# Attention and expert kernel: ScalarE presets the score banks with minus the row maxima

## Chip, cores and metric

One core of one Trainium2 chip. The time is device microseconds (us) of one execution of the whole program. Runs of the kernel before: 915.74, 917.42 and 919.55 us, median 917.42.

## What is computed

One transformer block in fp32, on x of 2 batches x 1024 tokens x 128 features: a modulated layer norm, attention with 16 heads of 64 (queries and keys over 64 latents, rotated by position), gates, a second layer norm, and an expert layer (8 experts, each token by one of its two best). The change lies in the attention alone:

```python
h = _layernorm(x, axis=-1) * (1 + ca) + sa
q = _apply_rope_subspace((c_q @ w_up_q.T) ..., DR)
k = _apply_rope_subspace((c_kv @ w_up_k.T) ..., DR)
scores = jnp.einsum('bhqd,bhkd->bhqk', q, k) * scale
attn = jax.nn.softmax(scores, axis=-1)
out = jnp.einsum('bhqk,bhkd->bhqd', attn, v)
out = out @ w_out.T + residual
```

## The kernel before

**Pairs, halves, steps.** The attention works through 16 pairs of heads (8 for each batch). A pair has 16 steps: two halves of 512 queries, and in each half eight tiles of 128 keys. Two steps are a group, so that a pair has eight groups, 0 to 7. Nothing schedules the work: each engine has its own queue, written out by hand in nested loops over p (pair) and g (group), and the queues meet through named semaphores.

**One group on TensorE.** `maxima(p + 1, 2g)` multiplies 128 queries of the next pair with 512 keys for both heads, into the two banks of `ps_m` (L411), for VectorE to reduce. `score(p, 2g)` and `score(p, 2g + 1)` each fill two banks of `ps_s`, scores transposed, keys on partitions: for both heads k_hi by q_hi (L429), k_lo by q_hi (L431), k_hi by q_lo (L433), and a row product (L435), ones by the row `neg_row`, that subtracts from each query its maximum. The first head lies on partitions 0 to 63 and the second on 64 to 127, so that the products come in twos. Then `maxima(p + 1, 2g + 1)`, `up(p + 2, g)` (L399, a quarter of a later pair's q or k), and `pv` for the two steps before (L445, probabilities by latent values, into `ps_o`). Steps of even number use banks 0 and 1 of `ps_s`, the odd ones banks 2 and 3.

In groups 3 and 7 there follow `denominators` (L453, ones by the sums of probabilities, into bank 2 of `ps_s`) and `outputs` (L462, of the pair before, into bank 3), which wait until `expo` has read the step's scores. So step 1 or 9 behind them waits until ScalarE has read the denominators and VectorE has added the outputs to `x_sb`.

**The other engines.** VectorE, in a group: `reduce_max` (L1082) of the first maxima, `lower` (L1075, the lower bits of the q or k quarter of the group before, which frees its banks for `up`), `reduce_max` of the second maxima, `turn` (L1064 to L1069, rotation). In groups 0 and 4 it begins with `out_add` (L1135) and ends with `recip` (L1121); in groups 3 and 7 it has `neg_max` (L1087, minus the maximum of a half's queries, in `nm`); in groups 2 and 6 `divide` (L1126). `maxima` waits until the reduction before has emptied `ps_m`; `up` waits for `lower`. ScalarE: `upper` (L676, a cast), `expo` twice (L684, the exponential of two banks, 128x1024), `den_out` (L696) at the start of groups 0 and 4, `o_out` (L691) at their end. GpSimd adds each step's probabilities (L930).

**SyncE's queue.** For each half, `max_rows` (L1377) sends the eight columns of `nm`, 128 numbers each, to `neg_row` by eight DMAs. `den_cols` (L1385), `inv_rows` (L1390) and `inv_spread` (L1395) take the denominators of a half to columns for `recip`, and the inverses over HBM to all partitions for `divide`. The queue is in order: `max_rows(p, 1)`, `den_cols(p - 1, 0)` and what follows it, `max_rows(p + 1, 0)`, `den_cols(p - 1, 1)` and what follows.

In pair 14 nothing is left for `up`, and in pair 15 nothing for `maxima`; there VectorE also has the second layer norm and the choice of experts for batch 0. The expert layer comes last.

Of the kernel before, what the change touches and what calls it, by code (L numbers as in the profile page):

```python
# [46 lines left out]
def build(nc, t, out):  # L47
    ctx = ExitStack()
    with ctx:
# [6 lines left out]
        def sem(name):  # L56
# [35 lines left out]
        one_row = sb("one_row", [P, P], F32R)  # L92
        neg_row = sb("neg_row", [P, 2, S], F32R)
# [3 lines left out]
        nm = sb("nm", [P, 2, 2, 4], F32R)  # L97
# [10 lines left out]

        rd_dram = nc.dram_tensor("rd_dram", [2, 2, HALF], F32, kind="Internal").ap()
# [97 lines left out]
            "scores": "both heads' scores of a step, less the maximum (tensor)",  # L207
# [38 lines left out]
        row_placed = [sem(f"row_placed{n}") for n in range(2)]  # L246
# [94 lines left out]
        def _(pe):  # L341
# [73 lines left out]
            def score(p, st):  # L415
# [4 lines left out]
                ge(pe, s["probs"], n_step(p, st) - 2)  # L420
                if kt == 0:
                    pe.wait_ge(row_placed[half], 128 * (p + 1))
                if kt == 1:
                    ge(pe, s["den_read"], n_part(p, half) - 2)
                    ge(pe, s["out_added"], n_part(p, half) - 3)
                kc, qc = slice(kt * P, (kt + 1) * P), slice(half * HALF, (half + 1) * HALF)
                bank = [ps_s[:, 2 * (st % 2) + h, :] for h in range(2)]
                for h in range(2):
                    nc.tensor.matmul(bank[h], k_hi[rows(h), p % 3, kc], q_hi[rows(h), p % 3, qc], start=True, stop=False)  # L429
                for h in range(2):  # L430
                    nc.tensor.matmul(bank[h], k_lo[rows(h), p % 3, kc], q_hi[rows(h), p % 3, qc], start=False, stop=False)  # L431
                for h in range(2):
                    nc.tensor.matmul(bank[h], k_hi[rows(h), p % 3, kc], q_lo[rows(h), p % 3, qc], start=False, stop=False)  # L433
                for h in range(2):
                    ins = nc.tensor.matmul(bank[h], one_row[rows(h), :], neg_row[rows(h), p % 2, qc], start=False, stop=True)  # L435
# [20 lines left out]
            def outputs(p, half, bank):  # L456
# [67 lines left out]
            for p in range(NPAIR):  # L524
                for g in range(NGRP):
# [95 lines left out]
        def _(act):  # L621
# [64 lines left out]

            def o_out(p, half):
# [60 lines left out]

            for p in range(NPAIR):
# [786 lines left out]
```

## Time and profile before

| | |
|---|---|
| median of three runs | 917.42 us |
| the profiled execution's own time | 909.34 us |
| its span, first to last instruction | 907.6 us |
| TensorE matmul busy | 818.4 us (90%), 5118 instructions |
| VectorE busy | 641.9 us (71%) |
| ScalarE busy | 394.1 us (43%) |
| GpSimd busy | 663.3 us (73%) |
| mean granted TensorE clock | 0.946 of full |
| chain that ended last: TensorE's part | 78% |

The span is what lies between the first and the last instruction of the profiled execution; that execution took 909.34 us, 1.7 us more than its span, and 8.1 us less than the median of the three runs without a profile. Busy time on TensorE is the union of its matmuls' times, whose ends are modelled. The attention lies between about 78 and 792 us; the expert layer follows.

### The profile page before, as it was taken

The page shows a single profiled execution, that of the slowest core. Times are in us where ns is not written, and L with a number is a line of the kernel's source. Part 1 is how long each engine was busy: PE and PEld are TensorE (multiplying, and loading weights), DVE is VectorE, ACT ScalarE, POOL GpSimd, SP SyncE. Part 2 cuts the span into 40 slices and gives each one's busy share as a digit, 9 for nine tenths or more (in the row PEclk, how much of TensorE's full clock was granted, in tenths as well). Part 3 has the DMA queues.
Part 4 walks back from the last instruction along what each step waited for, and adds up shares of the span by engine and source line. Part 5 has one row for each costly group of instructions (what it writes and reads, how often), then busy time and mean ns, then how long its engine had stood idle before and what let it go on. Part 6 is the DMA issues. An engine that isn't in the chain of part 4 may idle for free.

```text
span 907.6 us, 14678 instructions
## 1 busy us (share of the span) xinstructions
PE 818.4 (90%) x5118; PEld 489.8 (54%) x5118; DVE 641.9 (71%) x1156; ACT 394.1 (43%) x644; POOL 663.3 (73%) x350
## 2 busy tenths in 40 slices
PE   3678999999999999999999999999999977959591
PEld 1435555555555555555555555555555434448581
DVE  7877777777777777777777777777777767536023
ACT  2443444444444444444444444444444324326351
POOL 3684988888878787878788787878778866532433
PEclk8776999999999999999999999999999989869796
DMA  7200001010101010101011111010010100068693
GB/s 194 79 1 13 13 13 25 13 25 14 24 14 25 14 25 13 24 14 24 14 24 14 25 13 25 13 26 14 13 13 13 24 13 1 13 211 273 212 328 88
DMA packets 84330, 43.91 MB, mean 48 GB/s; under 512 B 57632, under 2 KB 73376, under 8 KB 84192
## 3 DMA queue, kind: packets, MB, share of 16 engines
q1 hardware_dynamic: 83232, 40.86, 17.6%
q0 software_dynamic: 1024, 2.10, 0.7%
q8 instruction: 42, 0.69, 0.3%
q14 instruction: 32, 0.26, 0.1%
HBM read 36.51 MB, written 6.16 MB: 47 GB/s over the span
## 4 chain that ended last, share of the span: by engine, by line
PE 78%; DVE 7%; DMA 5%; POOL 5%; issue 2%; ACT 1%; SPq 1%; POOLq 0%; DVEq 0%; ACTq 0%
PE ps_o L445 25%; PE ps_m L411 9%; PE ps_x L399 8%; PE ps_s L429 6%; PE ps_s L431 6%; PE ps_s L435 6%; PE ps_s L433 6%; PE ps_s L462 3%; DMA moe<-xs_dram 3%; PE ps_s L453 3%; POOL xs_dram L944 2%; DVE mx L1082 1%; PE ps_s L578 1%; PE ps_s L587 1%; DMA wu<-in_wqk 1%
## 5 line engine op out<-in xcount | busy, mean ns | idle before, releaser
L930 POOL TENSOR_TENSOR acc<-acc,probs 128x1024 f32<-128x1024 f32 (+1 forms) x192 | 459.7, 2394 | 80.4 <-ACT probs L684 58.0
L1082 DVE TENSOR_REDUCE mx<-ps_m 128x2 f32<-128x1024 f32 x240 | 293.8, 1224 | 92.8 <-PE ps_m L411 92.0
L684 ACT ACTIVATE probs<-ps_s 128x1024 f32<-128x1024 f32 x256 | 248.9, 1023 | 162.8 <-PE ps_s L435 162.8
L445 PE MATMUL ps_o<-probs,c_all 128*64 128x512 f32 x1024 | 249.7, 608 | 0.0
L930 POOL TENSOR_TENSOR acc<-probs 128x1024 f32<-128x1024 f32 (+1 forms) x32 | 75.2, 2351 | 57.5 <-ACT probs L684 56.9
L429 PE MATMUL ps_s<-q_hi,k_hi 64*128 64x512 f32 x512 | 103.1, 399 | 12.0 <-DVE x_sb L1135 12.0
L445 PEld LDWEIGHTS ps_o<-probs,c_all 128*64 128x64 f32 x1024 | 62.4, 136 | 93.2 <-issue 44.3
L411 PE MATMUL ps_m<-k_hi,q_hi 64*128 64x512 f32 x480 | 108.1, 446 | 3.7 <-DVE mx L1082 3.7
L431 PE MATMUL ps_s<-q_hi,k_lo 64*128 64x512 f32 x512 | 101.8, 394 | 0.0
L435 PE MATMUL ps_s<-neg_row,one_row 64*128 64x512 f32 x512 | 101.6, 393 | 0.0
L433 PE MATMUL ps_s<-q_lo,k_hi 64*128 64x512 f32 x512 | 101.0, 390 | 0.0
L411 PEld LDWEIGHTS ps_m<-k_hi,q_hi 64*128 64x128 f32 x480 | 46.2, 184 | 91.5 <-issue 81.4
L429 PEld LDWEIGHTS ps_s<-q_hi,k_hi 64*128 64x128 f32 x512 | 48.9, 187 | 24.3 <-issue 17.2
L1135 DVE TENSOR_TENSOR x_sb<-x_sb,ps_s 128x512 f32<-128x512 f32 x30 | 20.6, 688 | 49.8 <-PE ps_s L462 49.8
L433 PEld LDWEIGHTS ps_s<-q_lo,k_hi 64*128 64x128 f32 x512 | 48.9, 187 | 11.0
L435 PEld LDWEIGHTS ps_s<-neg_row,one_row 64*128 64x128 f32 x512 | 48.8, 186 | 11.1
L431 PEld LDWEIGHTS ps_s<-q_hi,k_lo 64*128 64x128 f32 x512 | 48.9, 187 | 10.7
L696 ACT COPY den<-ps_s 128x512 f32<-128x512 f32 x30 | 17.6, 586 | 77.6 <-PE ps_s L453 77.6
L1069 DVE TENSOR_TENSOR ps_x<-ps_x,tmp 128x256 f32<-128x256 f32 x112 | 48.4, 432 | 3.8
L676 ACT CAST q_hi<-ps_x 128x256 fp32r<-128x256 f32 x56 | 20.9, 374 | 66.7 <-DVE ps_x L1069 66.7
L1064 DVE TENSOR_TENSOR ps_x<-ps_x,rot 128x256 f32<-128x256 f32 x112 | 47.3, 423 | 0.0
L1067 DVE TENSOR_TENSOR tmp<-ps_x,rot 128x256 f32<-128x256 f32 (+1 forms) x113 | 47.2, 418 | 0.0
(289 smaller groups left out, 1034.2 us busy)
## 6 DMA issues: line engine op xcount, KB each, us to landing
probs<-in_experts SPq DMA_DIRECT2D x15, 578.0 KB, 5.4
rr<-rd_dram SPq DMA_DIRECT2D x62, 128.0 KB, 3.0
wu<-in_wqk SPq DMA_DIRECT2D x16, 256.0 KB, 3.1
neg_row<-nm SPq DMA_DIRECT2D x256, 0.5 KB, 2.0
w_first<-in_experts SPq DMA_DIRECT2D x5, 578.0 KB, 4.6
rot<-in_experts SPq DMA_DIRECT2D x5, 578.0 KB, 5.1
hT<-in_experts SPq DMA_DIRECT2D x5, 578.0 KB, 5.6
xs_dram<-zero SPq DMA_DIRECT2D x2, 960.0 KB, 6.8
```

The lines of the kernel that those rows point to most:

```text
L399: ins = nc.tensor.matmul(bank, m[:, q % 2, w, twin, :], src, start=(n == 0), stop=(n == 1))
L411: ins = nc.tensor.matmul(bank[:, h, :], q_hi[rows(h), q % 3, qt * P:(qt + 1) * P], k_hi[rows(h), q % 3, kh * HALF:(kh + 1) * HALF], start= ...
L429: nc.tensor.matmul(bank[h], k_hi[rows(h), p % 3, kc], q_hi[rows(h), p % 3, qc], start=True, stop=False)
L431: nc.tensor.matmul(bank[h], k_lo[rows(h), p % 3, kc], q_hi[rows(h), p % 3, qc], start=False, stop=False)
L433: nc.tensor.matmul(bank[h], k_hi[rows(h), p % 3, kc], q_lo[rows(h), p % 3, qc], start=False, stop=False)
L435: ins = nc.tensor.matmul(bank[h], one_row[rows(h), :], neg_row[rows(h), p % 2, qc], start=False, stop=True)
L445: ins = nc.tensor.matmul(ps_o[64 * h:64 * h + 64, :], c_all[:, (p // HP) * TB + kt, :], probs[:, st % 4, h, :], start=(kt == 0), stop=(kt ...
L684: nc.scalar.activation(probs[:, st % 4, :, :], ps_s[:, 2 * (st % 2):2 * (st % 2) + 2, :], ACT.Exp, scale=SCALE).then_inc(s["probs"], 1)
L930: V.tensor_tensor(acc[:, half, heads, :], first, probs[:, st % 4, heads, :], ALU.add).then_inc(s["added"], 1)
L1064: V.tensor_tensor(straight, straight, cos_sb[:, c], ALU.mult).then_inc(s["turned"], 1)
L1069: V.tensor_tensor(straight, straight, part, ALU.add).then_inc(s["rotated"], 1)
L1082: V.reduce_max(mx[:, :, kh, qt], max_banks(q, n), AX.X).then_inc(s["max_reduced"], 1)
```

## The change

ScalarE gets a new step, `preset`: a copy of 128x1024 from `neg_wide`, which holds minus the maxima of a half's queries on all partitions, into the two score banks of a step. The three products of `score` then accumulate onto it, with no first product that overwrites, and the row product and its tiles `one_row` and `neg_row` go. SyncE makes `neg_wide`: one DMA writes `nm` to HBM as rows, and two DMAs spread each head's row to 128 partitions. The waits of `score` for its bank, its row and the readers of banks 2 and 3 go to `preset`; `score` waits for `preset` alone. `outputs` has `start` only on the first of its four products. In groups 3 and 7 the denominators and outputs go between the two `pv`.

```diff
-        one_row = sb("one_row", [P, P], F32R)
-        neg_row = sb("neg_row", [P, 2, S], F32R)
+        neg_wide = sb("neg_wide", [P, 2, 2, HALF])
...
-                ge(pe, s["probs"], n_step(p, st) - 2)
-                if kt == 0:
-                    pe.wait_ge(row_placed[half], 128 * (p + 1))
-                if kt == 1:
-                    ge(pe, s["den_read"], n_part(p, half) - 2)
-                    ge(pe, s["out_added"], n_part(p, half) - 3)
+                pe.wait_ge(s["preset"], n_step(p, st))
...
-                    nc.tensor.matmul(bank[h], k_hi[rows(h), p % 3, kc], q_hi[rows(h), p % 3, qc], start=True, stop=False)
+                    nc.tensor.matmul(bank[h], k_hi[rows(h), p % 3, kc], q_hi[rows(h), p % 3, qc], start=False, stop=False, skip_group_check=True)
...
-                for h in range(2):
-                    ins = nc.tensor.matmul(bank[h], one_row[rows(h), :], neg_row[rows(h), p % 2, qc], start=False, stop=True)
...
-                                           g_all[:, p // HP, p % HP, :], start=True, stop=True)
+                                           g_all[:, p // HP, p % HP, :], start=(n == 0), stop=(n == 3))
...
-                    for n in (2 * g - 2, 2 * g - 1):
+                    def value_step(n):
                         if n >= 0:
                             pv(p, n)
                         elif p > 0:
                             pv(p - 1, NSTEP + n)
+
+                    value_step(2 * g - 2)
                     if g in (3, 7):
                         pe.wait_ge(s["probs"], n_step(p, 2 * g + 1))
...
+                    value_step(2 * g - 1)
...
+            def preset(p, st):
+
+                half, kt = divmod(st, TB)
+                if p == 0 and st < 2:
+                    act.wait_ge(s["max_reduced"], NMAX - 1 + st)
+                ge(act, s["probs"], n_step(p, st) - 2)
+                if kt == 0:
+                    act.wait_ge(row_wide[half], 32 * (p + 1))
+                if kt == 1:
+                    ge(act, s["den_read"], n_part(p, half) - 2)
+                    ge(act, s["out_added"], n_part(p, half) - 3)
+                nc.scalar.copy(ps_s[:, 2 * (st % 2):2 * (st % 2) + 2, :], neg_wide[:, half, :, :]).then_inc(s["preset"], 1)
...
+            preset(0, 0)
+            preset(0, 1)
             for p in range(NPAIR):
                 for g in range(NGRP):
                     if g == 0 and p > 0:
                         den_out(p - 1, 0, ps_s[:, 2, :])
+                        preset(p, 1)
                     if g == 4 and p > 0:
                         den_out(p - 1, 1, ps_s[:, 2, :])
+                    if g == 4:
+                        preset(p, 9)
...
                     expo(p, 2 * g)
                     expo(p, 2 * g + 1)
+                    if g < NGRP - 1:
+                        preset(p, 2 * g + 2)
+                        if g != 3:
+                            preset(p, 2 * g + 3)
+                    elif p < LAST:
+                        preset(p + 1, 0)
...
             def max_rows(q, half):
 
                 sp.wait_ge(s["max_row"], 2 * q + half + 1)
-                if q >= 2:
-                    sp.wait_ge(s["scores"], n_step(q - 2, TB * half + TB - 1))
+                sp.dma_start(mr_dram[half].rearrange("h (t p) -> p h t", p=P), nm[:, half, :, :],
+                             allow_slow_non_contiguous=True).then_inc(row_out[half], 16)
+
+            def max_spread(q, half):
+
+                sp.wait_ge(row_out[half], 16 * (q + 1))
+                if q:
+                    sp.wait_ge(s["preset"], n_step(q - 1, TB * half + TB - 1))
                 for h in range(2):
-                    for n in range(4):
-                        row = neg_row[64 * h:64 * h + 1, q % 2, half * HALF + n * P:half * HALF + (n + 1) * P]
-                        sp.dma_start(row.bitcast(F32), nm[:, half, h, n:n + 1].bitcast(F32)).then_inc(row_placed[half], 16)
+                    sp.dma_start(neg_wide[:, half, h, :],
+                                 mr_dram[half, h:h + 1, :].to_broadcast([P, HALF])).then_inc(row_wide[half], 16)
```

In the main loop of SyncE's queue `max_spread` stands directly behind each `max_rows`. Two places of the order follow.

TensorE, groups 3 and 7 in the middle of the attention, before (from the last score product of the group to the next group's maxima; ps_m are the maxima, ps_x the up projections, ps_o the value products, L453 the denominators, L462 the outputs):

```order
L435 MATMUL ps_s<-neg_row,one_row 128x512 x2
L411 MATMUL ps_m<-k_hi,q_hi 128x512 x2
L399 MATMUL ps_x<-ck,wh 128x256
L399 MATMUL ps_x<-ck,wl 128x256
L399 MATMUL ps_x<-ck,wh 128x256
L399 MATMUL ps_x<-ck,wl 128x256
L445 MATMUL ps_o<-probs,c_all 64x512 x4
L453 MATMUL ps_s<-acc,ones 64x512 x2
L462 MATMUL ps_s<-hT,ou 128x128 x4
L411 MATMUL ps_m<-k_hi,q_hi 128x512 x2
```

The same place after:

```order
L430 MATMUL ps_s<-q_lo,k_hi 128x512 x2
L413 MATMUL ps_m<-k_hi,q_hi 128x512 x2
L401 MATMUL ps_x<-ck,wh 128x256
L401 MATMUL ps_x<-ck,wl 128x256
L401 MATMUL ps_x<-ck,wh 128x256
L401 MATMUL ps_x<-ck,wl 128x256
L440 MATMUL ps_o<-probs,c_all 64x512 x2
L448 MATMUL ps_s<-acc,ones 64x512 x2
L457 MATMUL ps_s<-hT,ou 128x128 x4
L440 MATMUL ps_o<-probs,c_all 64x512 x2
L413 MATMUL ps_m<-k_hi,q_hi 128x512 x2
```

The row product is gone, and half of the value products now stands behind the outputs.

ScalarE, from a common group over a boundary between halves, before (probs are the exponentials, ps_x to q_hi or k_hi the casts):

```order
L676 CAST q_hi<-ps_x 128x256
L684 ACTIVATE probs<-ps_s 128x1024 x2
L696 COPY den<-ps_s 128x512
L676 CAST k_hi<-ps_x 128x256
L684 ACTIVATE probs<-ps_s 128x1024 x2
L691 COPY ou<-ps_o 128x512
```

The same place after (L696 is now the preset):

```order
L674 CAST q_hi<-ps_x 128x256
L682 ACTIVATE probs<-ps_s 128x1024 x2
L696 COPY ps_s<-neg_wide 128x1024
L707 COPY den<-ps_s 128x512
L696 COPY ps_s<-neg_wide 128x1024
L674 CAST q_hi<-ps_x 128x256
L682 ACTIVATE probs<-ps_s 128x1024 x2
L696 COPY ps_s<-neg_wide 128x1024 x2
L702 COPY ou<-ps_o 128x512
```

Each group has two presets behind its two exponentials; at the boundary the second of them stands behind the copy of the denominators and ahead of the cast and the next exponentials.

## Rows read from the trace of the kernel before

**Rows 1.** Windows: busy us of each engine, PEclk, DMA share, GB/s, in three stretches
```profile
110.00:700.00 590.00, 590.00 (x3742) 334.88 (x3740) 452.58 (x746) 273.62 (x374) 490.60 (x215) 1.00 0.10 18
705.00:715.00 10.00, 9.57 (x60) 4.71 (x58) 8.37 (x23) 4.31 (x5) 9.43 (x5) 1.00 0.03 5
735.00:745.00 10.00, 4.70 (x29) 3.04 (x26) 8.42 (x12) 1.61 (x2) 3.66 (x2) 0.78 0.09 1
```

**Rows 2.** Timeline of TensorE: start us, us, instructions [idle before <-releaser]; one whole group
```profile
417.42 0.50 PE L411 MATMUL ps_m<-k_hi,q_hi 64*128 64x512 f32 x2
417.75 0.39 PE L429 MATMUL ps_s<-q_hi,k_hi 64*128 64x512 f32 x2
...
418.45 0.40 PE L435 MATMUL ps_s<-neg_row,one_row 64*128 64x512 f32 x2
...
419.37 0.39 PE L435 MATMUL ps_s<-neg_row,one_row 64*128 64x512 f32 x2
419.59 0.39 PE L411 MATMUL ps_m<-k_hi,q_hi 64*128 64x512 f32 x2
419.91 0.38 PE L399 MATMUL ps_x<-cq,wh 128*128 128x256 f32 x1
...
420.58 1.94 PE L445 MATMUL ps_o<-probs,c_all 128*64 128x512 f32 x8
...
422.45 0.50 PE L411 MATMUL ps_m<-k_hi,q_hi 64*128 64x512 f32 x2
```

**Rows 3.** Timeline of VectorE in the same group
```profile
417.96 1.23 DVE L1082 TENSOR_REDUCE mx<-ps_m 128x2 f32<-128x1024 f32 x1 [0.61 <-PE ps_m L411]
419.10 0.42 DVE L1075 TENSOR_TENSOR q_lo<-ps_x,q_hi 128x256 fp32r<-128x256 f32 x1
420.02 1.23 DVE L1082 TENSOR_REDUCE mx<-ps_m 128x2 f32<-128x1024 f32 x1 [0.51 <-PE ps_m L411]
```

**Rows 4.** Timeline, VectorE and TensorE: where TensorE waited for VectorE
```profile
84.48 1.22 DVE L1082 TENSOR_REDUCE mx<-ps_m 128x2 f32<-128x1024 f32 x1
...
85.84 0.50 PE L411 MATMUL ps_m<-k_hi,q_hi 64*128 64x512 f32 x2
86.27 0.38 PE L399 MATMUL ps_x<-ck,wh 128*128 128x256 f32 x1
...
770.91 0.68 DVE L1135 TENSOR_TENSOR x_sb<-x_sb,ps_s 128x512 f32<-128x512 f32 x1
...
771.74 0.79 PE L429 MATMUL ps_s<-q_hi,k_hi 64*128 64x512 f32 x2 [5.63 <-DVE x_sb L1135]
```

**Rows 5.** Timeline of ScalarE in that group and at the next denominators
```profile
418.89 1.94 ACT L684 ACTIVATE probs<-ps_s 128x1024 f32<-128x1024 f32 x2 [1.13 <-PE ps_s L435]
...
428.45 0.59 ACT L696 COPY den<-ps_s 128x512 f32<-128x512 f32 x1 [2.59 <-PE ps_s L453]
428.93 0.38 ACT L676 CAST q_hi<-ps_x 128x256 fp32r<-128x256 f32 x1
```

**Rows 6.** Timeline, TensorE and VectorE, at the end of a half
```profile
428.33 1.16 PE L462 MATMUL ps_s<-hT,ou 128*128 128x128 f32 x8
429.42 0.50 PE L411 MATMUL ps_m<-k_hi,q_hi 64*128 64x512 f32 x2
...
429.53 0.69 DVE L1135 TENSOR_TENSOR x_sb<-x_sb,ps_s 128x512 f32<-128x512 f32 x1 [1.91 <-PE ps_s L462]
```

**Rows 7.** Timeline of SyncE's queue and VectorE, then DMA issues with us to landing
```profile
426.51 5.04 SPq L1377 DMA_DIRECT2D neg_row<-nm  x8
431.65 1.19 SPq L1385 DMA_DIRECT2D denc<-den  x2
...
434.32 0.20 DVE L1121 RECIPROCAL rc<-denc 128x8 f32<-128x8 f32 x1
...
ys_dram<-moe SPq DMA_DIRECT2D x10, 192.0 KB, 5.6
rd_dram<-rc SPq DMA_DIRECT2D x31, 4.0 KB, 1.8
```

More of the change, by code:

```diff
@@ L96, in build @@
         mx = sb("mx", [P, 2, 2, TB])
-        nm = sb("nm", [P, 2, 2, 4], F32R)
+        nm = sb("nm", [P, 2, 2, 4])
         den = sb("den", [P, HALF])
@@ L107, in build @@
         rt_sb = sb("rt_sb", [P, 12, TB * E])
+        mr_dram = nc.dram_tensor("mr_dram", [2, 2, HALF], F32, kind="Internal").ap()
         rd_dram = nc.dram_tensor("rd_dram", [2, 2, HALF], F32, kind="Internal").ap()
@@ L206, in build @@
             "max_row": "both heads' maxima of half the queries, negated (vector)",
-            "scores": "both heads' scores of a step, less the maximum (tensor)",
+            "preset": "a step's score banks hold minus the maximum (scalar)",
+            "scores": "both heads' scores of a step, added to it (tensor)",
             "probs": "their probabilities (scalar)",
@@ L245, in build @@
         up_in = sem("up_in")
-        row_placed = [sem(f"row_placed{n}") for n in range(2)]
+        row_out = [sem(f"row_out{n}") for n in range(2)]
+        row_wide = [sem(f"row_wide{n}") for n in range(2)]
         den_cols_in, inv_out, inv_in = sem("den_cols_in"), sem("inv_out"), sem("inv_in")
@@ L428, in score @@
                 for h in range(2):
-                    nc.tensor.matmul(bank[h], k_hi[rows(h), p % 3, kc], q_hi[rows(h), p % 3, qc], start=True, stop=False)
+                    nc.tensor.matmul(bank[h], k_hi[rows(h), p % 3, kc], q_hi[rows(h), p % 3, qc], start=False, stop=False, skip_group_check=True)
                 for h in range(2):
-                    nc.tensor.matmul(bank[h], k_lo[rows(h), p % 3, kc], q_hi[rows(h), p % 3, qc], start=False, stop=False)
+                    nc.tensor.matmul(bank[h], k_lo[rows(h), p % 3, kc], q_hi[rows(h), p % 3, qc], start=False, stop=False, skip_group_check=True)
                 for h in range(2):
-                    nc.tensor.matmul(bank[h], k_hi[rows(h), p % 3, kc], q_lo[rows(h), p % 3, qc], start=False, stop=False)
-                for h in range(2):
-                    ins = nc.tensor.matmul(bank[h], one_row[rows(h), :], neg_row[rows(h), p % 2, qc], start=False, stop=True)
+                    ins = nc.tensor.matmul(bank[h], k_hi[rows(h), p % 3, kc], q_lo[rows(h), p % 3, qc], start=False, stop=True, skip_group_check=True)
                 ins.then_inc(s["scores"], 1)
@@ L991, in then @@
                 dve.wait_ge(s["vector_step"], seq[0])
-            V.memset(ones[:], 1.0)
-            V.memset(one_row[:].bitcast(F32), 0.0)
-            then(V.memset(neg_row[:].bitcast(F32), 0.0))
-            V.memset(one_row[0:1, :].bitcast(F32), 1.0)
-            V.memset(one_row[64:65, :].bitcast(F32), 1.0).then_inc(s["constants"], 1)
+            V.memset(ones[:], 1.0).then_inc(s["constants"], 1)
             def statistics(src, tiles):
@@ L1085, in neg_max @@
                 dve.wait_ge(s["max_reduced"], NMAX * q + TB * (half + 1))
-                ge(dve, row_placed[half], 128 * q)
+                ge(dve, row_out[half], 16 * q)
                 V.tensor_reduce(nm[:, half, :, :], mx[:, :, :, 4 * half:4 * half + 4].rearrange("p h k t -> p h t k"),
@@ L1409, in _ @@
             weights(2)
-            sp.wait_ge(s["constants"], 1)
-            max_rows(0, 0)
-            max_rows(0, 1)
+            for half in range(2):
+                max_rows(0, half)
+                max_spread(0, half)
             weights(3)
@@ L1416, in _ @@
                 if p > 0:
-                    if p < LAST + 1:
-                        max_rows(p, 1)
+                    max_rows(p, 1)
+                    max_spread(p, 1)
                     den_cols(p - 1, 0)
@@ L1423, in _ @@
                     max_rows(p + 1, 0)
+                    max_spread(p + 1, 0)
                 if p > 0:
```

## The prediction

> **What bounds the kernel now.** I read four views, in this order. First the windows: from 110 to 700 us TensorE is busy for all of 590.00 us at the full granted clock (2.4 GHz), while ScalarE has 273.62 us of work and VectorE 452.58 [rows 1]. So in thirteen pairs TensorE's queue sets the pace, and a product taken out is worth its time until something else comes last. The question is what that is, and when. For this I laid the timeline of TensorE over one group [rows 2] and that of VectorE over the same group [rows 3]; then I looked for places where TensorE did wait for VectorE, for the price of the handover [rows 4]. Last come ScalarE and SyncE, which get the new work [rows 5 to 7].
>
> One group lasts from one first maxima product to the next, 417.42 to 422.45: 5.03 us [rows 2]. The eight twos of products of its two score steps lie between 417.75 and 419.59, so 0.23 us each. The second maxima products start 2.17 us after the first.
>
> **The row products.** Each group loses two of these twos, 0.46 us. Over 128 groups that would be 59 us, were TensorE alone to decide. It is not. The second maxima products go into the banks that VectorE reduces from 417.96 to 419.19 [rows 3], which is 1.77 us after the group's start. Now they come 0.40 us after that; without the row products they would be due 1.71 us after the start, 0.06 us before the reduction ends. The handover costs 0.14 to 0.15 us: a reduction ended at 85.70 and the products came at 85.84, an addition ended at 771.59 and the products came at 771.74 [rows 4]. So they start at 1.92. After such a wait the up projection followed 0.43 us later (85.84 to 86.27), against 0.32 without one (419.59 to 419.91) [rows 2, 4]; it now starts at 2.35 instead of 2.49. The lower bits that it also needs are there at 2.10 [rows 3], with the handover 2.25, so they don't come last. Everything behind is as before. **A group gains 0.14 us of its 0.46**, and TensorE gets a gap of about 0.3 us in each group. The reduction itself can't start sooner: it waits for its own products (0.61 us idle, [rows 3]).
>
> **The order at the half's end.** Groups 3 and 7 gain the same 0.14. Splitting the value products adds one change of product shape, for which rows 2 show 0.10 us at most (the maxima products behind value products take 0.33 us until the next, two score products 0.23). I take 0.05, with bounds 0 and 0.11. What the split buys: the output products end one half of the value products earlier. Now VectorE's addition starts 1.20 us after the outputs do, 0.11 us into the next group [rows 6], and delays the first reduction there; after, it is done 0.15 us before the group starts. So groups 0 and 4 gain the 0.14 too. **A pair gains 8 x 0.14 - 2 x 0.05 = 1.0 us, pairs 0 to 13 together 14 us.**
>
> **The presets.** ScalarE gets 256 copies of 128x1024 into PSUM. No row shows such a copy. From below: a copy of 128x512 takes a slot of 0.48 us, since the next instruction starts 0.48 us after it, so two are 0.96 [rows 5]; two exponentials of 128x1024 take 1.94, a slot of 0.92 and a duration of 1.02. From above: twice the whole 0.59 us of the 128x512 copy, 1.18. I take the exponential's, which has the same size. Counted from the group's start, the exponentials begin 1.24 us in (now 1.47, at 418.89; one two of products less), the presets follow at 3.1 and 4.0 and end at 5.0, the cast at 5.3, and the next exponential is due at 4.89 + 1.24 = 6.13. So 0.8 us are free, and the score products need their preset at 5.2 and 5.9. Hidden, unless a slot is over 1.3 us. At the half's end it is tight: the second bank's preset waits for VectorE's addition, which ends 0.15 us before the group; with 1.02 us and the handover that is 1.04 us into the group, and the step's products are due at 1.02. This is covered by the second maxima products, which VectorE holds back anyway; with 1.18 us per preset some 0.2 us come through at each of 30 half ends, 6 us in all. In pair 0 the exponential's table load may slip behind the first two presets, which costs a few tenths of a us against as much gained by shorter scores at 1.2 GHz: nothing.
>
> **SyncE.** Eight DMA issues of 5.04 us [rows 7] go, one DMA and two broad ones come. No row has a write of 1,024 single numbers to HBM. The nearest are 1.8 us for 256 runs of four numbers and 5.6 us for the expert rows of 192 KB, both to HBM [rows 7]; I take 2.5, near the first, as it is as small. Then the denominators' DMAs are issued at about 426.4 + 2.5 + 1.2 = 430.1 instead of 431.65. That pays for 0.5 MB of spreading ahead of them in the queue. Nothing. The spread rows themselves have some 20 us until they are used.
>
> **The last two pairs.** In pair 14 VectorE alone comes last in two groups (between 705 and 715 it is busy for 8.37 of 10 us, [rows 1]), the rest gain 0.12 each, 0.7 in all. Three times TensorE stands still for VectorE's late addition, the longest for 5.63 us [rows 4]; there the preset now comes between addition and products: 3 x 1.1 = 3.3 us lost. Steps behind it get some 2 us back from the shorter scores. Net 0.5 us lost. The constants' fills that go at the start lie beside input DMAs: nothing.
>
> **The sum.** 14 - 0.5 = 13.5 us. The profiled execution of 909.3 us would come to 895.8. It lies 8.1 us under the median of the three runs, 917.42; taken from the median, the forecast is **904 us**. With the bounds (presets of 1.18 us: 6 us back; no split cost: 1.5 us more; handovers 0.03 us shorter per group: 4 us more) it spans 898 to 911. Under 912.8 or over 922.0, half a per cent, is what a measurement of this kernel can tell from no change.
>
> **Rivals.**
>
> 1. TensorE gains all it loses: the reduction doesn't hold it. For it: no wait for VectorE shows in the steady groups. Against it: rows 2 and 3 put the reduction's end 0.06 us behind the time at which its products would be due. 917.4 - 59 + 4 for the last pairs: 862 us. Chance 0.04.
>
> 2. The half ends eat the gain. If the second bank's preset comes later than I reckon (the addition 0.3 us later, or a handover through ScalarE slower), TensorE waits about 0.45 us at each of 30 half ends: 13.5 us, so 917 us. For it: at that place the slack is nothing. Chance 0.09.
>
> 3. ScalarE becomes the bound. A group asks of it a cast, two exponentials and two presets: 0.3 + 1.84 + 2 presets. That passes 5.03 us from 1.45 us per preset on. At 1.5 us: 128 x 0.11 = 14 us slower, 931 us. Against it: no row of this size comes near. Chance 0.05.
>
> 4. **The slow side: the denominators come late.** SyncE waits for its write to land before it may spread, and `den_cols` stands behind. From the issue of these DMAs to the reciprocal at 434.32 there are 2.7 us now [rows 7]. Behind the reciprocal, which ends at 434.52, VectorE is idle until the next group's reduction at 434.99 (429.42 + 5.03 + 0.54, [rows 2, 3, 6]); that leaves 0.47 us, less 0.28 for two groups that get 0.14 shorter. So 426.4 + landing + 1.2 + 2.7 must not pass 434.5, and it decides from a landing of 4.2 us on, or less, as the 0.5 MB stand in the way. Landing at 5.6, VectorE stalls for 1.4 us in 30 halves, and TensorE with it: 904 + 42 = 946 us. For it: a write of single numbers; against it: the eight DMAs now move as many single numbers in 5.04 us, in a stage whose DMA share is 0.10 [rows 1, 7]. The Trainium skill (DMA: Bandwidth & Descriptors, section Rules for kernel authors) says that a strided last dimension lowers to one descriptor per element, and that one should rearrange; by this rule the write is the slowest form there is, and this rival would hold. No run here shows it yet. Chance 0.07.
>
> 5. The clock. A gap in every group could bring the granted clock down to 1.2 GHz at times; if for a tenth of the 590 us, 59 us are added: 963 us. Against it: between 705 and 715 TensorE was busy for 9.57 of 10 us, with gaps much like those to come, and had the full clock; it fell only where it was busy for 4.70 of 10 us, to a mean of 0.78 [rows 1]. The Trainium skill (TensorE: Matmul & The Clock Gate, section A second HAM failure mode: psum-queue depth-cycling) tells of a kernel whose short frequent idles made the clock swing; by that rule the time would be this rival's, and the window from 705 speaks against it here. Chance 0.03.
>
> **How the numbers follow.** The forecast has 0.72. Of it 0.02 may land within half a per cent, as may rival 2; faster has 0.70 and rival 1's 0.04, so 0.74; same 0.11; slower 0.15 (rivals 3 to 5). The range reaches from 895 to 919: the forecast's own 898 to 911, three us below it, and above it rival 2. Outside remain rival 1 and the slow ones, 0.19.
>
> **What would show it.** Right: a group of 4.89 us in the middle; the second maxima products 1.92 us behind the first, with VectorE's reduction named as what TensorE waits for, some 0.3 us per group; a half's end shorter by 0.1; presets of about 1.0 us whose end no score product waits for, outside the last two pairs; the clock at 1.00 from 110 to 690; the reciprocal not waiting for DMAs. Wrong: a group of 4.6 us (rival 1); score products waiting for presets in the middle (2, 3); VectorE idle ahead of the reciprocal (4); matmul starts 0.43 us apart (5).

## The result and the profile after

| | before | after |
|---|---|---|
| median | 917.69 us (915.74 to 919.55, 4 runs) | 1156.76 us (1155.32 to 1160.29, 4 runs) |
| ratio after to before, 95% interval | | 1.261 (1.258 to 1.265) |
| span | 907.6 us | 1155.2 us |
| TensorE busy | 818.4 us (90%) | 873.8 us (76%) |
| ScalarE busy | 394.1 us | 630.5 us |
| mean granted TensorE clock | 0.946 | 0.848 |

The forecast was 904 us; the change costs 239 us. TensorE was rid of some 59 us of row products (the prediction's estimate, 0.46 us in 128 groups) and is nevertheless busy for 55 us more, and idle for 192 us more (1155.2 - 873.8 = 281, against 89 before).

The page of the kernel after; columns: share of the chain by line; then busy us, mean ns | idle us before, releaser:

```profile
PEclk7779888888888888888888888899998888887787
...
DMA mr_dram<-nm 23%; PE ps_o L440 14%; DMA denc<-den 9%; PE ps_m L413 7%; DVE mx L1100 7%; PE ps_x L401 4%; PE ps_s L426 3%; PE ps_s L428 3%; SPq L1399 3%; PE ps_s L430 3%; PE ps_s L576 2%; PE ps_s L585 2%; SPq L1408 1%; DMA wu<-in_wqk 1%; DVE hn L1186 1%
...
L696 ACT COPY ps_s<-neg_wide 128x1024 f32<-128x1024 f32 x256 | 254.4, 1029 | 61.3 <-DVE x_sb L1153 53.5
L413 PE MATMUL ps_m<-k_hi,q_hi 64*128 64x512 f32 x480 | 131.7, 538 | 188.2 <-DVE mx L1100 186.4
...
L1139 DVE RECIPROCAL rc<-denc 128x8 f32<-128x8 f32 x31 | 6.3, 202 | 205.2 <-DMA denc<-den 205.2
```

The new write of the maxima, `mr_dram<-nm`, is the largest item of the chain that ended last. VectorE stood for 205 us ahead of its 31 reciprocals, and TensorE for 186 us ahead of maxima products: that is nearly all of the 192 us of new idle time, one wait handed on. One such place, timelines of SyncE, VectorE and TensorE in the kernel after (start us, us, [idle before <-releaser]):

```profile
513.27 0.37 SPq L1390 DMA_DIRECT2D mr_dram<-nm  x1
521.83 0.81 SPq L1399 DMA_DIRECT2D neg_wide<-mr_dram  x2
522.75 1.15 SPq L1408 DMA_DIRECT2D denc<-den  x2
...
527.86 0.20 DVE L1139 RECIPROCAL rc<-denc 128x8 f32<-128x8 f32 x1 [6.73 <-DMA denc<-den]
527.98 1.18 DVE L1100 TENSOR_REDUCE mx<-ps_m 128x2 f32<-128x1024 f32 x1
...
529.31 0.79 PE L413 MATMUL ps_m<-k_hi,q_hi 64*128 64x512 f32 x2 [6.22 <-DVE mx L1100]
...
531.18 3.68 PE L440 MATMUL ps_o<-probs,c_all 128*64 128x512 f32 x8
```

The write goes out at 513.27 and the spread, which waits for its landing (the signal that the data have arrived), at 521.83: 8.56 us. From write to spread it is 8.5 to 8.8 us in the first eighteen halves that have columns behind them, 9.5 in the next, and 10.0 to 11.4 in the last ten. Then the denominators' columns follow, and the reciprocal starts 5.11 us behind their issue, where it was 2.67 before (431.65 to 434.32, [rows 7]). 0.5 MB of spreading stand ahead of them in the queue, but that is only part of the reason, as experiment 6 will show. VectorE takes its work in order, so the reduction behind the reciprocal is late, and with it the banks of the maxima. The value products that follow take 3.68 us for eight, where [rows 2] had 1.94. The windows of the same kernel around the stall (columns as in [rows 1]):

```profile
522.00:528.00 6.00, 1.09 (x10) 0.56 (x6) 0.14 (x2) 3.98 (x5) 4.40 (x3) 0.77 0.38 88
528.00:534.70 6.70, 5.39 (x14) 2.01 (x14) 3.83 (x7) 0.37 (x1) 0.37 (x1) 0.50 0.28 79
```

A granted clock of 0.50 is the lower level, 1.2 GHz: TensorE had been busy for 1.09 of the 6 us before, and got the lower level when it went on. In the 6 us behind each of the 19 stalls of this kind between 110 and 700 us the granted clock was 0.50 to 0.72.

Between the stalls the kernel does what was forecast. TensorE, two groups of the kernel after (compare [rows 2]):

```profile
509.36 0.50 PE L413 MATMUL ps_m<-k_hi,q_hi 64*128 64x512 f32 x2
...
511.27 0.50 PE L413 MATMUL ps_m<-k_hi,q_hi 64*128 64x512 f32 x2
511.70 0.39 PE L401 MATMUL ps_x<-ck,wh 128*128 128x256 f32 x1
...
516.33 0.51 PE L413 MATMUL ps_m<-k_hi,q_hi 64*128 64x512 f32 x2
...
521.21 0.50 PE L413 MATMUL ps_m<-k_hi,q_hi 64*128 64x512 f32 x2
```

The group from 516.33 lasts 4.88 us (5.03 before), the second maxima products stand 1.91 us behind the first and the projection 0.43 behind them.

### The profile page after: what moved, and what is told of

Its sections match the earlier page's. It is cut to its first block, busy times and chain, and to the rows that moved or that the text cites. A ratio compares the mean times of both kernels' runs of the same rounds, so it can differ in the third digit from the quotient of the medians.

```text
span 1155.2 us, 13764 instructions
## 1 busy us (share of the span) xinstructions
PE 873.8 (76%) x4606; PEld 468.9 (41%) x4606; DVE 640.3 (55%) x1152; ACT 630.5 (55%) x900; POOL 662.6 (57%) x350
## 3 DMA queue, kind: packets, MB, share of 16 engines
q0 software_dynamic: 1024, 2.10, 0.5%
## 4 chain that ended last, share of the span: by engine, by line
PE 40%; DMA 33%; DVE 13%; SPq 5%; issue 4%; POOL 3%; ACT 2%; POOLq 0%; ACTq 0%; DVEq 0%
DMA mr_dram<-nm 23%; PE ps_o L440 14%; DMA denc<-den 9%; PE ps_m L413 7%; DVE mx L1100 7%; PE ps_x L401 4%; PE ps_s L426 3%; PE ps_s L428 3%; SPq L1399 3%; PE ps_s L430 3%; PE ps_s L576 2%; PE ps_s L585 2%; SPq L1408 1%; DMA wu<-in_wqk 1%; DVE hn L1186 1%
## 5 line engine op out<-in xcount | busy, mean ns | idle before, releaser
L440 PE MATMUL ps_o<-probs,c_all 128*64 128x512 f32 x1024 | 302.3, 708 | 0.0
L696 ACT COPY ps_s<-neg_wide 128x1024 f32<-128x1024 f32 x256 | 254.4, 1029 | 61.3 <-DVE x_sb L1153 53.5
L413 PE MATMUL ps_m<-k_hi,q_hi 64*128 64x512 f32 x480 | 131.7, 538 | 188.2 <-DVE mx L1100 186.4
L413 PEld LDWEIGHTS ps_m<-k_hi,q_hi 64*128 64x128 f32 x480 | 52.8, 202 | 348.6 <-issue 347.4
L426 PE MATMUL ps_s<-q_hi,k_hi 64*128 64x512 f32 x512 | 106.7, 412 | 19.1 <-ACT ps_s L696 19.0
L1139 DVE RECIPROCAL rc<-denc 128x8 f32<-128x8 f32 x31 | 6.3, 202 | 205.2 <-DMA denc<-den 205.2
L440 PEld LDWEIGHTS ps_o<-probs,c_all 128*64 128x64 f32 x1024 | 67.9, 154 | 101.7 <-issue 68.7
L674 ACT CAST k_hi<-ps_x 128x256 fp32r<-128x256 f32 x56 | 21.0, 375 | 86.8 <-DVE ps_x L1087 86.8
L401 PE MATMUL ps_x<-cq,wh 128*128 128x256 f32 (+1 forms) x114 | 40.7, 374 | 0.0
```

Of the source, the lines that this page charges most:

```text
L401: ins = nc.tensor.matmul(bank, m[:, q % 2, w, twin, :], src, start=(n == 0), stop=(n == 1))
L413: ins = nc.tensor.matmul(bank[:, h, :], q_hi[rows(h), q % 3, qt * P:(qt + 1) * P], k_hi[rows(h), q % 3, kh * HALF:(kh + 1) * HALF], start= ...
L440: ins = nc.tensor.matmul(ps_o[64 * h:64 * h + 64, :], c_all[:, (p // HP) * TB + kt, :], probs[:, st % 4, h, :], start=(kt == 0), stop=(kt ...
L696: nc.scalar.copy(ps_s[:, 2 * (st % 2):2 * (st % 2) + 2, :], neg_wide[:, half, :, :]).then_inc(s["preset"], 1)
```

## The experiments

Two questions were asked. Is the slow write the whole loss, and why is it slow? And what is the rest of the change worth without it?

### 1. The denominators ahead of the spread

```diff
                 if p > 0:
                     max_rows(p, 1)
-                    max_spread(p, 1)
                     den_cols(p - 1, 0)
+                    max_spread(p, 1)
```

(The same for the other half.)

> The changed kernel, with SyncE's queue reordered alone: den_cols goes ahead of max_spread, so the denominators' DMAs no longer wait for the landing of the write of single numbers. Theory A (the wait for that landing, some 8.5 us, in front of den_cols, is the whole loss): VectorE no longer waits for denc ahead of the reciprocal (205 us before), a group takes 4.88 us, the clock is 1.00 in the middle, time about 904 us, at most 1.0 us above that per half if the later spreads come late for divide. Theory B (the load of the spreads, 0.5 MB per half and 16 MB in all, slows the small DMAs of the queue): the stall falls by less than half, time over 1030 us. Theory C (the presets or the clock lose the time by themselves): over 1100 us.

Measured: 1017.96 us against 917.81, a ratio of 1.109 (1.105 to 1.112). VectorE's wait for the columns in this kernel (us in total, times, longest):

```profile
DVE rc L1139 <- DMA denc<-den: 64.6, 22, 5.4
```

And its timeline, SyncE and VectorE:

```profile
512.78 0.38 SPq L1390 DMA_DIRECT2D mr_dram<-nm  x1
516.70 1.15 SPq L1408 DMA_DIRECT2D denc<-den  x2
...
524.56 0.20 DVE L1139 RECIPROCAL rc<-denc 128x8 f32<-128x8 f32 x1 [1.18 <-DMA denc<-den]
```

139 us came back, so the place of the wait matters, but 100 stayed: more than theory A allows, and under what B and C expected. The columns were issued at 516.70, with no wait for the write, and the reciprocal still came 7.9 us later (6.1 to 11.1 us over all halves). What stands behind the slow write in the queue is signalled late too, whether or not the program waits for it: the columns lie in SBUF at both ends, and the trace has their last packet at 519.0, more than 5 us ahead of the reciprocal.

### 2. Only the row product goes

The kernel before, without the product at L435 (and a scale of 0 in the exponential):

```diff
-                for h in range(2):
-                    ins = nc.tensor.matmul(bank[h], one_row[rows(h), :], neg_row[rows(h), p % 2, qc], start=False, stop=True)
```

> The kernel before without the row product L435 and with nothing in its place; the exponentials' scale is 0, so that they can't overflow. What TensorE alone gets from the removal, with VectorE's chain of reductions as it is. My account (VectorE's reduction holds the second maxima products): a group takes 4.89 us instead of 5.03, the middle 1.1 us less per pair, the whole about 15 to 20 us less (pair 15 has no maxima and gains up to 3.7). Rival (TensorE alone sets the pace): a group takes 4.57 us and the whole is 55 to 59 us less.

Measured: 903.17 us, a ratio of 0.983 (0.979 to 0.987), 14.6 us gained, just under the 15 to 20 expected and far from the rival's 55 to 59. TensorE in one group of this kernel, and VectorE's reduction of the first maxima:

```profile
409.75 0.50 PE L411 MATMUL ps_m<-k_hi,q_hi 64*128 64x512 f32 x2
...
410.30 1.23 DVE L1080 TENSOR_REDUCE mx<-ps_m 128x2 f32<-128x1024 f32 x1 [0.61 <-PE ps_m L411]
...
411.67 0.50 PE L411 MATMUL ps_m<-k_hi,q_hi 64*128 64x512 f32 x2
412.10 0.38 PE L399 MATMUL ps_x<-cq,wh 128*128 128x256 f32 x1
...
414.63 0.50 PE L411 MATMUL ps_m<-k_hi,q_hi 64*128 64x512 f32 x2
```

1.92, 0.43, 4.88: with no preset and no split at all, a group gets shorter by only 0.15 of the 0.46 us that its two row products took. The reduction ends at 411.53 and the second maxima products start 0.14 us later, at 411.67, the handover of [rows 4]: they are held by VectorE's reduction.

### 3. Only the write comes

The kernel before, with the write of the maxima to HBM and a wait for it ahead of `den_cols`; the row DMAs go behind `inv_spread`. No preset, no spread, the row product stays.

```diff
+            def write_rows(q, half):
+                sp.wait_ge(s["max_row"], 2 * q + half + 1)
+                sp.dma_start(mr_dram[half].rearrange("h (t p) -> p h t", p=P), nm[:, half, :, :].bitcast(F32),
+                             allow_slow_non_contiguous=True).then_inc(row_out[half], 16)
+                sp.wait_ge(row_out[half], 16 * q)
...
-                        max_rows(p, 1)
+                    write_rows(p, 1)
                     den_cols(p - 1, 0)
...
+                    max_rows(p, 1)
```

> The kernel before, with one thing of the change: from pair 1 on a write of nm to HBM as rows (1,024 single numbers) and a wait for its landing ahead of den_cols; the eight row DMAs stand behind inv_spread. No preset, no spread, row products as before. Theory A: VectorE waits some 6 us ahead of 30 reciprocals and the clock falls behind each wait, time 1130 to 1200 us. Theory B (the spreads' load): the wait is under 2 us, time below 975 us. Theory C: as before, 917 us.

Measured: 1098.83 us, a ratio of 1.196 (1.191 to 1.201). This lies 31 us under the lower end of the 1130 to 1200 us expected, and far above theories B and C. One write and one wait, added to the kernel before, bring 181 of the 239 us. VectorE's waits for the columns sum up to 152.7 us. One of them in the timeline of SyncE and VectorE:

```profile
518.39 0.36 SPq L1383 DMA_DIRECT2D mr_dram<-nm  x1
529.89 1.17 SPq L1393 DMA_DIRECT2D denc<-den  x2
...
532.53 0.20 DVE L1123 RECIPROCAL rc<-denc 128x8 f32<-128x8 f32 x1 [6.28 <-DMA denc<-den]
```

With the write landed and no spreads ahead of them, the columns are used after the old 2.6 us here (529.89 to 532.53). In return the write took 11.5 us at this place; from half to half it is 8.7 to 11.7 us until the columns' issue, and VectorE's wait 3.5 to 6.5. So less is lost than in the changed kernel above all in the halves where the write takes under 10 us, and hardly less at a place like this one. What makes it take 9 us or 11 the runs don't show.

### 4 and 5. What makes the write slow

Small DMAs out of columns of numbers behind the kernel's end, one after another, each waited for, with nothing else moving. First, 1,024 single numbers as eight rows of 128 neighbours (full), two such rows (two), the same 1,024 as 128 runs of eight (runs), eight DMAs of 128 singles (rows), and the same eight into SBUF (neg_row):

```diff
+            def timed(*dmas):
+                for dst, src in dmas:
+                    sp.dma_start(dst, src, allow_slow_non_contiguous=True).then_inc(probed, 16)
+                    count[0] += 16
+                sp.wait_ge(probed, count[0])
```

> The kernel before, with DMAs measured by themselves behind the result's store, three times each, one after the other's landing: full_hbm, the write of 1,024 single numbers to HBM as in the change; two_hbm, the same form with 256 single numbers; runs_hbm, the same 1,024 numbers as 128 runs of eight; rows_hbm, eight DMAs of 128 single numbers to HBM; neg_row, eight of them within SBUF. If the count of single numbers at one issue sets the landing: full_hbm 8 to 9 us, two_hbm 3 to 4, runs_hbm about 2, rows_hbm and neg_row about 2 behind the last issue. If the trip to HBM sets it: all the hbm forms over 5 us. If it is load in the attention: all about 2 us.

DMA issues of that kernel: count, KB each, median us to landing:

```profile
neg_row<-nm SPq DMA_DIRECT2D x280, 0.5 KB, 2.0
...
full_hbm<-nm SPq DMA_DIRECT2D x3, 4.0 KB, 8.8
two_hbm<-nm SPq DMA_DIRECT2D x3, 1.0 KB, 8.0
runs_hbm<-nm SPq DMA_DIRECT2D x3, 4.0 KB, 1.4
rows_hbm<-nm SPq DMA_DIRECT2D x24, 0.5 KB, 6.4
```

A quarter of the numbers lands hardly sooner (3 to 4 us were expected if the count set the time), so the count is not the cause. Cut into eight DMAs it gets no better: 6.4 us each, 10 to 11 us from the first issue to the last landing. As runs of eight the same bytes land in 1.4 us, so the way to HBM is not it, and singles into SBUF take 2.0. With no other traffic it is as slow as in the kernel. Left over is single numbers in HBM, and there is one more question: any singles, or neighbours? So the second look takes 128 numbers side by side (near), 512 bytes apart (far) and 64 bytes apart (fine), then 128 runs of two and of four numbers, runs side by side (pair, quad).

> The kernel before, with DMAs to HBM behind the result's store, each waited for, three times: near_hbm, 128 single numbers side by side; far_hbm, 128 single numbers 512 B apart; fine_hbm, 128 single numbers 64 B apart; pair_hbm and quad_hbm, 128 runs of two and of four numbers side by side. If neighbours written by different engines hold each other up: near 6 us or more, far about 2, fine between, pair about 4, quad under 2. If a write of four bytes is slow by itself: near and far alike at 6 us or more.

DMA issues of the second kernel:

```profile
near_hbm<-nm SPq DMA_DIRECT2D x3, 0.5 KB, 8.0
far_hbm<-nm SPq DMA_DIRECT2D x3, 0.5 KB, 1.4
fine_hbm<-nm SPq DMA_DIRECT2D x3, 0.5 KB, 1.4
pair_hbm<-nm SPq DMA_DIRECT2D x3, 1.0 KB, 3.1
```

And SyncE's queue there, where each issue waits for the landing before it:

```profile
922.75 0.32 SPq L1490 DMA_DIRECT2D quad_hbm<-nm  x1
924.97 0.32 SPq L1490 DMA_DIRECT2D near_hbm<-nm  x1
```

128 single numbers take 8.0 us side by side and 1.4 us at 64 bytes apart, as short as at 512. With runs of two it is 3.1 us, with runs of four 2.2 (922.75 to 924.97; 1.8 in the next round), with runs of eight 1.4. So what costs is many small writes close to each other. How close isn't settled: runs of eight put two writes into each 64 bytes and cost nothing extra, so the stretch that counts may be 32 bytes as well as 64. The rest came near to what was expected, but for the numbers 64 bytes apart, which are no slower than those at 512. And the time isn't spent in moving the numbers: of the side-by-side write issued at 924.97, the trace has all packets done by 926.0, as soon behind the issue as for the spaced ones, and the DMA engines' busy share from 926.1 to 932.9 is 0.00. What comes late is the landing. That neighbouring writes are completed one after another would explain it, but the runs show only the addresses' effect.

### 6. The changed kernel with the write spaced out

If that is the whole cause, the changed kernel must run as forecast when only the addresses of its write differ. The write goes to a place that nobody reads, the spread reads zero rows, and the exponential has a scale of 0. So two more things differ beside the addresses: the probabilities are all one value, and the spread reads rows that weren't just written. Experiment 7 has neither of these differences.

```diff
-                sp.dma_start(mr_dram[half].rearrange("h (t p) -> p h t", p=P), nm[:, half, :, :],
+                sp.dma_start(mr_far[half, :, 0].rearrange("(h t p) -> p h t", p=P, h=2), nm[:, half, :, :],
```

> The changed kernel with its own order and waits in SyncE's queue, den_cols behind the write and the spread as there. Only the addresses of the write differ: the 1,024 numbers go to HBM 64 bytes apart, to a place that nobody reads. The spread reads the same number of bytes from rows that are zero, and the exponential has a scale of 0: the subtraction of the maxima is left out, the work is not. Theory A (only neighbouring single numbers land late, and nothing else in the changed kernel costs time): issue of the write to issue of the spread 1.4 to 3 us instead of 8.6, the denominators' DMAs go out early, the reciprocal waits under 0.5 us, groups 4.88, the clock full from 110 to 690, total as the run with rows made in SBUF or a little less, 892 to 908 us. Rival B (the wait for a landing ahead of den_cols costs in itself, or the spreads of 0.5 MB ahead of it do): the reciprocal still waits 1 us or more per half, 930 to 1000 us. Rival C (the write of 1,024 single numbers is slow among other traffic wherever it goes): landing 6 to 9 us again and 1130 to 1160 us.

Measured: 903.99 us against 917.27, a ratio of 0.984 (0.980 to 0.989). The middle of this kernel in the windows (columns as in [rows 1]):

```profile
110.00:690.00 580.00, 577.12 (x3328) 294.48 (x3324) 456.94 (x747) 472.48 (x592) 492.55 (x216) 1.00 0.17 43
```

And its timeline, SyncE and VectorE:

```profile
505.78 0.38 SPq L1392 DMA_DIRECT2D mr_far<-nm  x1
508.47 0.80 SPq L1401 DMA_DIRECT2D neg_wide<-mr_dram  x2
509.37 1.15 SPq L1410 DMA_DIRECT2D denc<-den  x2
...
513.55 0.19 DVE L1141 RECIPROCAL rc<-denc 128x8 f32<-128x8 f32 x1
```

As many single numbers, the same order and the same waits: 2.7 us from the write to the spread, a reciprocal that waits for nothing (0.9 us in the whole kernel), the full clock, and 253 us less. In both kernels the write's packets are done 1.6 us after its issue; only the landing differs. This is theory A; B and C are out. It also gives the split of the loss: the changed kernel's span is 249.8 us longer than this one's, with 182 us more in waits for the maxima (186.4 against 4.3) and 69.6 more in busy TensorE (873.8 against 804.2, for the same 4,606 products), which fits the lower clock behind the stalls; the other waits differ by little.

The columns stand behind the same 0.5 MB of spreads here. In the two halves where the reciprocal did wait for them it came 3.3 and 3.6 us behind their issue, not 5.1. So the spreads account for 0.6 to 0.9 us of the 2.4 that the changed kernel has over 2.67. There the spreads themselves start late: their first packets come 2.6 us behind their issue at 521.83, here 0.95. Why something is still held up after the write's landing is open.

### 7. A version that computes everything

The maxima go to SBUF rows by eight DMAs as before, `den_cols` directly behind them; from there two rows of 2 KB are written to HBM and spread, behind `inv_spread`.

```diff
+                for h in range(2):
+                    for n in range(4):
+                        sp.dma_start(neg_row[64 * h:64 * h + 1, half, n * P:(n + 1) * P],
+                                     nm[:, half, h, n:n + 1]).then_inc(row_out[half], 16)
...
+                for h in range(2):
+                    sp.dma_start(mr_dram[half, h:h + 1, :], neg_row[64 * h:64 * h + 1, half, :]).then_inc(row_stored[half], 16)
```

> The changed kernel with another way for the rows: eight DMAs of 128 single numbers within SBUF, as before the change, then two rows of 2 KB to HBM, then the two spreads; no write of single numbers to HBM. den_cols goes directly behind the eight, the store ahead of inv_rows, the spreads behind inv_spread. Theory A' (the slow write of single numbers to HBM is the whole loss: what waits for it, and the small DMAs that stand behind it in the queue, as in the run with the order alone): no wait ahead of the reciprocal of over 1 us in the middle, group 4.88 us, clock 1.00, time 898 to 908 us, which is my forecast without its failed term. Theory B (spreads of 0.5 MB per half slow the small DMAs): waits ahead of reciprocal or divide stay at several us, time over 950 us.

Measured: 899.11 us against 911.06 on the same chip, a ratio of 0.987 (0.985 to 0.990): 12.0 us faster than the kernel before, and the fastest version that computes the whole. TensorE of this kernel, two groups, the first with the denominators and outputs:

```profile
500.57 0.50 PE L415 MATMUL ps_m<-k_hi,q_hi 64*128 64x512 f32 x2
...
503.58 1.08 PE L442 MATMUL ps_o<-probs,c_all 128*64 128x512 f32 x4
504.49 1.03 PE L450 MATMUL ps_s<-acc,ones 128*64 128x512 f32 x4
...
506.54 1.08 PE L442 MATMUL ps_o<-probs,c_all 128*64 128x512 f32 x4
507.55 0.50 PE L415 MATMUL ps_m<-k_hi,q_hi 64*128 64x512 f32 x2
...
512.42 0.50 PE L415 MATMUL ps_m<-k_hi,q_hi 64*128 64x512 f32 x2
```

It subtracts the maxima, reads rows just written, and has the reciprocal wait for 2.2 us in all; the clock is 1.00 from 110 to 690. The common group takes 4.87 us. The one at the half's end takes 6.98, and in the kernel before 6.97 (422.45 to 429.42, [rows 2, 6]).

### 8. The split undone

The version of experiment 7 with both value products ahead of the denominators.

```diff
                     value_step(2 * g - 2)
+                    value_step(2 * g - 1)
                     if g in (3, 7):
...
-                    value_step(2 * g - 1)
```

> The kernel of e5_rows_in_sbuf with both value products ahead of the denominators again, as before the change. If the split does what I reckoned (VectorE's addition ends before the group, so that the second bank's preset is ready in time): without it the products of steps 1 and 9 come 0.9 us late at 30 half ends, time 25 to 30 us over e5_rows_in_sbuf. Rival (the preset is covered anyway): within 5 us of it.

Measured: 913.74 us, a ratio of 1.003 (1.001 to 1.006), and 14.6 us over experiment 7 on the same chip: half of what was expected. ScalarE and TensorE of this kernel behind the outputs:

```profile
520.08 1.02 ACT L698 COPY ps_s<-neg_wide 128x1024 f32<-128x1024 f32 x1 [1.29 <-DVE x_sb L1155]
...
521.15 0.50 PE L428 MATMUL ps_s<-q_hi,k_hi 64*128 64x512 f32 x2 [0.79 <-ACT ps_s L698]
```

Outputs, addition, preset and products come in a row here: TensorE waits 0.8 us at the half's end. I had not taken off what the unsplit group saves. It takes 6.83 us (512.34 to 519.17) against 6.98, so the net is nearer 0.6 us in 28 places.

### 9. The second maxima later

If VectorE's reduction holds the second maxima, TensorE could do half of the value products first. The version of experiment 7, with `maxima(p + 1, 2g + 1)` and `up` behind the first `value_step`.

> The kernel of e5_rows_in_sbuf, with TensorE's second maxima products and up moved behind the first of the two value products of a group. My account of the 0.46 us (VectorE's reduction holds back the second maxima products by 0.2 us, and the up projection by 0.1 more): now these come 2.6 us after the group's start, after the reduction; a common group takes 4.57 us, groups 2 and 6 some 0.4 more as divide delays the next reduction; time 870 to 885 us. Rival (ScalarE or GpSimd come last as soon as TensorE is faster): 895 us or more.

Measured: 947.45 us, a ratio of 1.039 (1.036 to 1.042). A miss: 48 us slower than experiment 7. Timelines of GpSimd, VectorE and TensorE of this kernel:

```profile
508.68 2.40 POOL L954 TENSOR_TENSOR acc<-acc,probs 128x1024 f32<-128x1024 f32 x1
...
509.31 2.31 DVE L1146 TENSOR_TENSOR ou<-ou,rr 128x512 f32<-128x512 f32 x1
...
512.90 0.50 PE L415 MATMUL ps_m<-k_hi,q_hi 64*128 64x512 f32 x2 [1.39 <-DVE mx L1102]
```

All its 31 divisions together (ns min/median/max, first and last start):

```profile
L1146 DVE TENSOR_TENSOR ou<-ou,rr x31: 675/2319/2601, 134.0 to 836.7; 128x512 f32<-128x512 f32 x31
```

Two things went wrong. The gap ahead of the second maxima is gone, since the value products now start 1.81 us behind the group's start and the second maxima at 2.82. But the value products in two pieces take 2.02 us instead of 1.87, so that a group without a stall lasts 4.92 us (503.70 to 508.62), not less than 4.87. The up projection also follows the maxima by 0.42 us here, though the maxima waited for nothing, so the wait isn't the only thing that makes 0.43 out of 0.32. And the division, whose operands both lie in SBUF, takes 2.3 us where it took 0.73 in experiment 7. In both kernels it starts while GpSimd adds; what differs is where in the addition. In experiment 7 it starts at 500.40, 0.18 us before an addition ends (498.20 to 500.58), here at 509.31, 1.77 us before (508.68 to 511.08), and in both it ends 0.54 us or so after that addition. Its mean rose from 0.78 to 2.08 us, 40 us over 31 divisions, and the waits for the reduction from 3.6 to 41.5 us. The Trainium skill (SBUF — State Buffer, section SBUF: two separate sides) describes a port pair that a VectorE operation with two SBUF inputs and a GpSimd operation hold by turns, each for a whole instruction. The trace agrees: the division ends as if it had started with the addition's end, and the excess, 1.9 us at most (2.60 - 0.68), is less than one addition of 2.4 us.

## Why the prediction was wrong, point by point

**The step that failed is the SyncE term**: "I take 2.5, near the first, as it is as small ... Nothing." The landing took 8.56 us at the place read in the kernel after (up to 11.4 elsewhere), 8.8 alone. The sum put it at nothing; the changed kernel against the one with the spaced write (experiment 6) shows 253 us in its place. I had bounded an operation that no row shows by the two nearest rows, 1.8 and 5.6 us, and both were of another kind: runs of four numbers 16 bytes long and expert rows of 512 bytes. Neither end covered it. Size was the wrong likeness; what counted was how many small pieces lie close together. The range of 895 to 919 us left out 1157 by far, and the right mechanism, rival 4, had a chance of 0.07.

**Rival 4** named the place, the queue, the condition (from 4.2 us on) and who waits. It was priced at 946 us, for a landing of 5.6. With 8.56 its own formula gives 426.4 + 8.56 + 1.2 + 2.7 - 434.5 = 4.4 us in 30 halves: 904 + 131 = 1035 us. Two terms of it were missing. The columns come 5.1 us behind their issue instead of 2.7, which makes stalls of some 6 us and 182 us in waits. And the products behind such a stall ran at the lower clock, 70 us more. Together 904 + 182 + 70 = 1156. This is bookkeeping against experiment 6, which happened to measure 904 itself, and no second forecast.

**The rule of the Trainium skill** on a strided last dimension (DMA: Bandwidth & Descriptors, section Rules for kernel authors), by which this rival would hold, led to the right outcome here, and the trace agrees on the pieces: 1,040 packets between the write's issue and the spread's. But their count does not set the time: the same 1,040 packets with the numbers 64 bytes apart landed in 2.7 us inside the kernel.

**The clock, rival 5.** The small gap in every group did no harm: 1.00 from 110 to 690 in experiment 6, with TensorE busy for 577 of 580 us. The clock did fall in the kernel after, but behind the stalls, to 0.50. My 963 us had the wrong trigger.

**The group: right.** The kernel after has 4.88 us against 4.89, second maxima at 1.91 against 1.92, projection at 2.34 against 2.35. Experiment 2 shows the cause: the same numbers without any preset. Rival 1 (862 us) is out. The gap doesn't stand in the list of waits as a wait for the reduction: only 4.3 us are booked there in experiment 6, and the starts of the products must be read.

**The half's end: the size off.** The split costs 0.16 us, not 0.05, and lies above my bound of 0.11: the value products take 0.91 + 1.01 us in two pieces (503.58 to 504.49, 506.54 to 507.55) and 1.76 in one (425.61 to 427.37 in the kernel before). So this group gained nothing instead of 0.09. The benefit was read rightly: without the split 14.6 us are lost (experiment 8), and with it the preset is nearly in time (in experiment 7 the second two products of step 1 start 0.27 us behind the first two, where 0.23 is normal). Rival 2 (917 us) is out.

**The presets: right.** 1.03 us (1.02 forecast) and hidden in the middle. Rival 3 needed 1.45 and is out.

**The sum** without its failed term: 14 - 0.5 = 13.5 us forecast; 13.3 in experiment 6, 12.0 in experiment 7. A pair is 6 x 0.15 - 2 x 0.01 = 0.88 us shorter, 12.3 over fourteen, which leaves about nothing for the last two pairs.

## What to carry to other kernels

Where a change adds a DMA of a shape that no row of the trace shows, and a wait for it stands ahead of something that has a deadline, its price is open upwards: look first at how late it may land (here 4.2 us), measure that shape by itself, and until then give the late case a real chance. To turn columns into rows, don't write single numbers side by side to HBM; go through SBUF (experiment 7), or write runs of 32 bytes (1.4 us alone, not tried in the kernel). And count more than its length for a stall like these: behind stalls of some 6 us TensorE's products ran at a granted clock of 0.50 to 0.72.

## What the chip showed that was not expected

- 128 numbers of 4 bytes land in HBM in 8.0 us side by side, in 1.4 us at 64 or 512 bytes apart; runs of 8, 16 and 32 bytes side by side take 3.1, 2.2 and 1.4 us. 1,024 numbers side by side take 8.8 us, hardly more than 128. In each of these forms of 128 the packets are done 1.0 us after the issue; the rest passes with the DMA engines at rest.
- Small DMAs behind such a write in the queue are late as well, though their packets have gone: 6.1 to 11.1 us from issue to use instead of 2.7 (experiment 1).
- Behind a stall of 6.2 us TensorE's granted clock was 0.50 over the next 6.7 us read; gaps of 0.2 us in every 4.88 left it at 1.00.
- A division of 128x512 took 2.3 us instead of 0.73 when it started early in one of GpSimd's additions instead of late in it (experiments 9 and 7).
